# Projections: the next head's four weight chunks split at token tiles 0, 1, 3 and 4 instead of 0, 2, 4 and 6

## The reference, cut to what matters

```python
q = jnp.einsum('bsd,ed->bse', x, Wq).reshape(bsz, seqlen, HQ, D)
k = jnp.einsum('bsd,ed->bse', x, Wk).reshape(bsz, seqlen, HK, D)
v = jnp.einsum('bsd,ed->bse', x, Wv).reshape(bsz, seqlen, HK, D)
q = _rmsnorm(q, q_norm_w)
k = _rmsnorm(k, k_norm_w)
...
q = _rope(q, pos)
k = _rope(k, pos)
```

## Time and profile before

| | us |
|---|---|
| device time, median of 3 runs | 1436.67 |
| lowest and highest of them | 1432.88, 1438.29 |
| the profiled execution's own time | 1433.48 |
| its span, first to last instruction | 1431.8 |
| PE busy in the span | 1328.7 |
| projections, first product to last transposes | 124.91 to about 483 |

### The profile page before, as it was taken

One profiled execution on the slowest core, in us unless ns is written; L12 is line 12 of the kernel. 1 busy time (PEld: TensorE's weight loads), 2 busy tenths in 40 slices (PEclk: granted clock), 3 DMA queues, 4 the chain that ended last, 5 costly groups with the idle time before them and its releaser, 6 DMA issues. The chain is left out here.

```text
span 1431.8 us, 30173 instructions
## 1 busy us (share of the span) xinstructions
PE 1328.7 (93%) x8584; PEld 1147.8 (80%) x8584; DVE 924.3 (65%) x2550; ACT 750.9 (52%) x1825; POOL 743.7 (52%) x737
## 2 busy tenths in 40 slices
PE   5988889888898599999999999999999999579999
PEld 3735778777787489999999999998999999468887
DVE  4696576655764477777777777777777777532222
ACT  2074343333433367777777777776777777421211
POOL 2032797777977666656666666655566564000000
PEclk9999999999999789999999999999999999799999
DMA  9213243324423899889888898988888893553341
GB/s 305 83 38 111 71 129 110 110 71 116 121 69 85 244 278 249 243 241 259 235 253 239 243 261 228 259 237 227 239 238 256 233 263 95 175 177 109 127 128 63
DMA packets 256499, 258.26 MB, mean 180 GB/s; under 512 B 57509, under 2 KB 218021, under 8 KB 256454
## 3 DMA queue, kind: packets, MB, share of 16 engines
q1 hardware_dynamic: 246406, 232.46, 56.4%
q0 software_dynamic: 9472, 25.21, 6.4%
q10 hardware_dynamic: 576, 0.05, 0.1%
HBM read 211.49 MB, written 46.14 MB: 180 GB/s over the span
## 5 line engine op out<-in xcount | busy, mean ns | idle before, releaser
L1046 DVE CUSTOM_DVE_ANT_1 att_neg<-att_mask,att_ps 128x576 f32<-128x576 f32 x256 | 193.1, 754 | 152.6 <-PE att_ps L95 152.5
L939 POOL TENSOR_TENSOR att_k_lo<-att_kT,att_k_hi 128x544 fp32r<-128x544 f32 x128 | 173.3, 1354 | 142.2 <-ACT att_k_hi L1148 142.2
L939 POOL TENSOR_TENSOR att_k_lo<-all_room_a,att_k_hi 128x544 fp32r<-128x544 f32 x128 | 174.3, 1363 | 133.5 <-ACT att_k_hi L1148 133.5
L93 PE MATMUL prj_ps<-prj_wt_hi,early_xT_lo 128*128 128x512 f32 (+1 forms) x512 | 186.7, 365 | 34.0 <-DVE prj_wt_lo L730 34.0
L1133 ACT ACTIVATE att_prob<-att_neg,att_nmax 128x544 f32<-128x544 f32 x256 | 191.6, 748 | 28.6 <-DVE att_nmax L1046 5.9
L1139 ACT ACTIVATE att_pT<-att_pb 128x256 f32<-128x256 f32 x256 | 98.5, 385 | 181.4 <-PE att_pb L979 181.4
L93 PE MATMUL att_ps<-att_k_hi,att_q_lo 128*128 128x288 f32 (+1 forms) x512 | 171.0, 334 | 11.8 <-POOL att_k_lo L939 11.8
L94 PE MATMUL prj_ps<-prj_wt_lo,early_xT_hi 128*128 128x512 f32 (+1 forms) x512 | 180.6, 353 | 0.0
L95 PE MATMUL prj_ps<-prj_wt_hi,early_xT_hi 128*128 128x512 f32 (+1 forms) x512 | 178.7, 349 | 0.0
L695 ACT ACTIVATE prj_sq<-prj_ps 128x512 f32<-128x512 f32 x64 | 38.3, 599 | 226.4 <-PE prj_ps L95 226.4
L95 PE MATMUL att_ps<-att_k_hi,att_q_hi 128*128 128x288 f32 (+1 forms) x512 | 148.7, 290 | 0.0
(11 more groups left out here) (146 smaller groups left out, 3360.4 us busy)
## 6 DMA issues: line engine op xcount, KB each, us to landing
all_room_a<-in_k_cache_t SPq DMA_DIRECT2D x256, 128.0 KB, 3.8
att_kT<-in_k_cache_t SPq DMA_DIRECT2D x256, 128.0 KB, 3.4
all_room_b<-in_L_cond_v_cache SPq DMA_DIRECT2D x160, 128.0 KB, 3.1
att_vc<-in_L_cond_v_cache SPq DMA_DIRECT2D x160, 128.0 KB, 3.2
q_scratch<-prj_qst SPq DMA_DIRECT2D x64, 256.0 KB, 2.2
o_scratch<-att_ost SPq DMA_DIRECT2D x32, 512.0 KB, 4.5
out_o_n<-o_scratch SPq DMA_DIRECT2D x32, 512.0 KB, 3.4
all_room_b<-in_L_cond_v_cache POOLq DMA_DIRECT2D x96, 128.0 KB, 3.9
```

The lines of the kernel that those rows point to most:

```text
L93: pe.matmul(out, w_lo, x_hi, start=first, stop=False)
L939: g.tensor_tensor(k_lo[j % SPLITS][:], kT[j // HK % 2][:, :, j % HK, :], f32(k_hi[j % SPLITS][:]), ALU.subtract).then_inc(k_split, 1)
L1046: v.tensor_tensor_reduce(halves[0], halves[1], ps[j % 2][:, :, 0:KA], 1.0, 3.0e38, ALU.add, ALU.min, nmax[j % 2][:]).then_inc(maxed, 1)
```

## The change

The bodies that carry a chunk become t = 0, 1, 3 and 4, and the chunk's number is looked up in a table. Nothing is added or removed: each head still has four high and four low parts, in the same buffers, with the same semaphores and counts.

```diff
+        SPLIT_AT = {0: 0, 1: 1, 3: 2, 4: 3}
+
         def split_at(t, last_head):
 
-            return t % 2 == 0 and not last_head
+            return t in SPLIT_AT and not last_head
...
                         if t == 0:
                             act.wait_ge(w_in[1 - slot], (it + 1 + slot) * 16)
-                        k = t // 2
+                        k = SPLIT_AT[t]
                         act.activation(wt_hi[1 - slot][:, k, :], wn[1 - slot][:, k, :], ACT.Copy).then_inc(w_hi_done, 1)
...
-                        k = t // 2
+                        k = SPLIT_AT[t]
                         split_lo(k, 1 - slot, (c + 1) * KC + k + 1)
```

## The result

| | before | changed |
|---|---|---|
| device time, median of 4 runs | 1434.78 us | 1390.04 us |
| lowest to highest | 1430.6 to 1438.29 | 1388.8 to 1392.28 |
| profiled execution, its own time | 1433.48 | 1388.88 |
| its span | 1431.8 | 1387.2 |

The ratio is 0.9691, with a 95% interval of 0.9659 to 0.9724: 44.7 us faster. The forecast was 1391.3.

A forecast was written before the change was run, and what follows sets the result against it. PE was taken to bound the kernel. Removing 27.8 us of head-change waits and 17.6 of slow clock, 45.4 in all, gave 1436.67 - 45.4 = 1391.3 us, range 1385 to 1399, chance 0.87.

The forecast's parts named there:

- What bounds the kernel: Projections: PE busy 93% of the span; seven head-change waits of 3.97 us for DVE's fourth low part would go.
- The sum: Seven head-change tiles in the projections, 78.75 us, would take 33.3, a gain of 45.4 us: 27.8 waits, 17.6 slow clock.
- The clock's part: PE's half-speed stretches after idling at the seven head changes would go, giving 17.6 us.
- the list of signs: Expected in the trace: one low-part wait of 6.2 us, transposes 4.76 us apart, clock 1.00, last head's first product at 391 us.
- rival 1: Head-change waits go but half-speed stretches come elsewhere on PE; only 27.8 us return, 1408.9 us; chance 0.05.
- rival 2: In the projections' heads, low parts in a row hold POOL 1.83 us, POOL becomes the bound, 1414 us; chance 0.04.
- The step-by-step count for head 0: POOL in head 0: tile 2 done at 148.19, tile 5 at 162.43, 1.3 us before its transposes; cost zero.
- rival 3: In the projections, DVE's low parts wait a whole POOL tile, 3.08 us more each; slower, 1478 us; chance 0.02.
- The prediction's bounds: DVE's low parts in the changed projections would take 1.8 to 2.2 us.
- ACT and SP: In the projections, ACT's moved high parts of 0.86 us and SP's weight loads and stores would cost zero.

## Why the prediction was right, point by point

**What bounds the kernel.** Seven waits of 3.97 us at the head changes, due to the fourth low part, and no other PE wait inside the stage: right. The change removed all seven and no other wait appeared; moving only the fourth chunk gives the whole gain, moving only the others gives none.

**The sum.** 45.4 us: the projections became 45.24 us shorter. That sum was read as a whole from the head changes, so it holds however it is divided. Its division into 27.8 us of waits and 17.6 of slow clock was off by some 1.7: a wait delays PE by 4.21 us and not by the 3.97 of the list, seven make 29.5, and 15.9 are left for the clock. Filling the idle time brought 15.8 back, with the wait still there. The clock's part rested on the slow stretches lying right behind the waits, and it is the part that a reader of the list of waits alone would have missed; it is about a third of the gain. For the profiled execution 1388.1 was forecast and 1388.88 measured; 0.55 of the difference is the later start of the stage.

**Two moments in the list of signs.** The last head's first product was put at 436 - 45 = 391 us and came at 393.44. The slow stretch of the seventh head change lies behind that product, and so its clock's part can't be taken off there. And the transposes are 4.76 us apart up to the 62nd tile, not to the last. Neither touches the forecast.

**The clock elsewhere (rival 1).** No slow stretch appeared between 131 us, where that of the very first product ends, and 431, where the last products end:

```profile
131.00:431.00 300.00, 300.00 (x1829) 267.26 (x1829) 215.04 (x469) 125.80 (x339) 278.89 (x251) 1.00 0.44 120
```

By the rule of the Trainium skill ("TensorE: Matmul & The Clock Gate", "What's actually happening"), that activity releases the throttle, nothing was to take the place of the slow stretches; the trace agrees, with 1.00 over these 300 us.

**POOL (rival 2).** The step-by-step count for head 0 came out within 0.01 us of the trace. The changed kernel's stage began 0.75 us later there (its tile 2 starts on POOL at 143.91, where the kernel before had 143.16), and with that taken off, tile 2 was to be done at 148.19 and was at 148.18, tile 5 at 162.43 and was at 162.42. POOL in tiles 2 and 5 of the changed kernel:

```profile
143.91 2.27 POOL L782 TENSOR_TENSOR prj_ta<-prj_ta,prj_tb 128x640 f32<-128x640 f32 x1
...
147.67 1.26 POOL L792 TENSOR_TENSOR prj_qn<-prj_ta,prj_rstd 128x640 f32<-128x640 f32 x1
...
161.91 1.26 POOL L792 TENSOR_TENSOR prj_qn<-prj_ta,prj_rstd 128x640 f32<-128x640 f32 x1
```

```profile
164.50 0.71 PE L680 MATMUL prj_pt<-all_ident,prj_qn 128*128 128x128 f32 x5
```

147.67 + 1.26 = 148.93, and 161.91 + 1.26 = 163.17; the transposes of tile 5 start at 164.50, 1.3 us later, as counted. In the other heads POOL falls back twice and is level again:

```profile
176.28 1.57 POOL L782 TENSOR_TENSOR prj_ta<-prj_ta,prj_tb 128x640 f32<-128x640 f32 x1 [0.29 <-DVE prj_tb L755]
...
181.27 1.57 POOL L782 TENSOR_TENSOR prj_ta<-prj_ta,prj_tb 128x640 f32<-128x640 f32 x1
...
186.26 1.56 POOL L782 TENSOR_TENSOR prj_ta<-prj_ta,prj_tb 128x640 f32<-128x640 f32 x1
...
190.56 1.57 POOL L782 TENSOR_TENSOR prj_ta<-prj_ta,prj_tb 128x640 f32<-128x640 f32 x1
```

4.99, 4.99, then 4.30: 190.56 is three times 4.76 behind 176.28, so POOL is level again. The margin is real and small: with the operation on all eight tiles POOL does become the bound.

**DVE starved (rival 3).** The case that the trace of before didn't hold, a low part that asks while POOL goes from one tile straight into the next, came in head 0. DVE was not starved; it got in first:

```profile
143.66 1.10 DVE L732 TENSOR_TENSOR prj_wt_lo<-prj_wn,prj_wt_hi 128x768 fp32r<-128x768 f32 x1
145.74 0.29 DVE L749 TENSOR_TENSOR prj_ta<-prj_ps,early_tabs 128x128 f32<-128x128 f32 x1 [0.98 <-PE prj_ps L95]
```

The low part took 1.10 us, since it only had to wait for the end of POOL's scaling, and it was POOL's addition that took 2.27 instead of 1.57. The prediction's bounds, low parts of 1.8 to 2.2 us, missed the short ones of 0.97 to 1.2 in head 0: which engine waits depends on how late POOL is. The sum for POOL is the same either way, 0.70 here and 0.71 there, which is why the miss changed nothing. That is the exclusion for a whole instruction of the Trainium skill ("SBUF — State Buffer", "Who interferes with whom"), both ways round.

**ACT and SP.** No wait for either before the last head's last two tiles, where PE waits 1.3 us for ACT as it did before; zero was right.

## What to carry to other kernels

A wait that comes back at each turn of an outer loop is often not a lack of throughput: look at whether the piece that is late is written into the same body that needs it, and move that one piece by one body; then count the engine that shares its time with it, tile by tile, for the slack that remains. Price an idle TensorE at more than the idle time, by the tile that follows it in the windows: here a wait that the list gives as 3.97 us took 6.5 us. Where a wait can't be removed, useless matmuls in it can give back the clock's part, 15.8 us here. When two placements give the same time, compare how early the piece is done before it is wanted, here 0.16 us and 5 us.

## What was new about the hardware

When DVE's two-input operation and a POOL operation meet, which one waits depends on who is first. Behind POOL's addition, DVE's 0.95 us becomes 1.8 to 2.05 (2.34 at the most, with four in a row) and POOL's next small step goes from 0.20 to 0.91, so both pay. With POOL later, DVE takes 0.97 to 1.2 and POOL's addition goes from 1.57 to 2.27, so nearly all of it is POOL's. POOL's running back to back did not keep DVE out. And the slow clock's length after equal waits of 3.96 us varied from tile to tile, from 5.76 to 6.98 us of lost time per head change with the wait included, while with the idle time filled down to 0.31 us it did not come at all.
